# The last phase of a two-layer MetaFormer block: where its second norm and its last bias are computed

## The chip, the cores and the metric

The kernel runs on one core of a Trainium2 chip. A core has five engines with queues of their own: TensorE (PE, matmuls; PEld is its loading of weights), VectorE (DVE), ScalarE (ACT), GpSimd (POOL) and SyncE (SP, which issues the DMAs here). Each engine works through its own program in order and waits on semaphores that other engines raise. The metric is the device time of one execution in microseconds. One execution is also recorded by the hardware profiler, and all rows below are from such a record.

## The reference

Two layers on `x` of shape (8, 96, 128, 128), each a token mixer with a channel norm and a residual, then a feed-forward part with its own norm and a residual:

```python
x = x + conv(_ln_c(x))                 # layer 0 clusters, layer 1 gates with depthwise convolutions
t = _to_tokens(x)
t = t + ffn(_ln_t(t), W1, b1, W2, b2)
x = _from_tokens(t, x)

def _ln_t(v, eps=1e-5):
    m = jnp.mean(v, axis=-1, keepdims=True); s = jnp.var(v, axis=-1, keepdims=True)
    return (v - m) / jnp.sqrt(s + eps)

def _qlinear(x, W, b):                 # q_mul: round to fp8 (5 exponent, 2 mantissa bits); q_acc: to f16
    y = q_acc(jnp.einsum('bsk,nk->bsn', q_mul(x), q_mul(W)))
    return q_acc(y + q_mul(b))

def ffn(x, W1, b1, W2, b2):
    return _qlinear(jax.nn.relu(_qlinear(x, W1, b1)), W2, b2)
```

So the norm's result is rounded to fp8 before the first layer, the second layer's product is rounded to f16, and its bias is added and rounded to f16 again.

## The kernel before, in words

Three phases follow one another. Phase A is layer 0 with the norm of layer 1; phase B the depthwise convolutions of layer 1; phase C, which the change touches, finishes layer 1: the pointwise convolution, the gate, the residual, and the feed-forward part of 96 to 384 to 96 channels.

Phase C works on units. A unit is a quarter of an image, 32 rows of 128 pixels or 4096 tokens; there are 32. A unit is cut into NK = 8 groups of 512 tokens, and a group is four tiles of 128 tokens (TPC = 4). The body of every engine runs over units, and in each over nine steps s = 0 to 8. In a step two units are at work. For the unit q = i + 1, the front: `mix` (L1645, the pointwise matmul), `gate` (L1725, DVE), `turn` (L1654, transposes to tokens), `x4` (L1735, the residual), `stats` (L178, mean and variance of each token, two instructions a group). For the unit i, the back: `pe_q8` (L1476, transposes the normed fp8 tokens), `act_q8` (L296), `pe_hidden` and `act_hidden` (L348, L361, three slices of 512 columns through two PSUM buffers), `dve_hidden` (L369 three times, bias and relu; L373, the rounding to fp8), `pe_y` (L1490, three matmuls), `act_y` (L1503, out of PSUM into f16), `dve_y` (L1509, the bias), `c_turn` (L1664) and `out` (L1754, the residual sum, which goes to memory by half units).

The order on each engine is the order of the code in `body`. In a step s TensorE does q8 of group s + 1, hidden slices 0 and 1 of group s, mix of group s of the next unit, hidden slice 2, turn, c_turn and y of group s - 1. ACT does q8c of group s + 1, the three hidden copies of group s, one norm group, and y of group s - 1. DVE does relu and round of group s, gate of s, x4 of s - 1, the bias of s - 1, statistics of s - 1, out of s - 1.

The norm. For each half unit (four groups) POOL turns the variance into 1/std and -mean/std (`norm_terms`, L1794 to L1801: var, less, a power, a product). ACT applies it, four activations of 128x96 a group, with scale and bias per token (`act_norm`, L1461). The table `LN_AT` (L1430) says in which step which group is normed: groups 0 to 2 of the next unit in steps 6, 7 and 8, group 3 in step 0, groups 4 to 7 in steps 2 to 5.

Two rings of PSUM banks tie the engines. A bank of the back ring (four banks; uses in the order q8, c, y) is taken again four uses later, so y of a group waits for `out` of the group before it. A bank of the front ring (two banks; pw, turn) is taken again two uses later, so `mix` of a group waits for `gate` of the group before. The third hidden slice takes the buffer that ACT's copy of the first slice frees.

Of the kernel before, what the change touches and what calls it, by code (L numbers as in the profile page):

```python
# [5 lines left out]
F32 = mybir.dt.float32  # L6
# [175 lines left out]
def per_token(t, n):  # L182

    return t.unsqueeze(2).to_broadcast([P, n, C])


class FeedForward:
# [47 lines left out]
    def dve_y(self, dve, i, k):  # L235
        ev = self.ev

        dve.wait_ge(ev["y16"], ev.at("y16", i, k))
        y = self.y16[:, k % 2, :].rearrange("p (t c) -> p t c", c=C)
        dve.tensor_tensor(self.y16b[:, k % 2, :].rearrange("p (t c) -> p t c", c=C), y,  # L240
                          self.w["b2"][:].unsqueeze(1).to_broadcast([P, TPC, C]), ALU.add).then_inc(ev["yb"], 1)
        dve.wait_ge(ev["yb"], ev.at("yb", i, k))
        x = self.x_of(i)[:, k * CW:(k + 1) * CW]
        dve.tensor_tensor(x, x, self.y16b[:, k % 2, :], ALU.add).then_inc(ev["x2"], 1)
# [1184 lines left out]
            channels(dve, body)  # L1429


LN_AT = {6: (1, 0), 7: (1, 1), 8: (1, 2), 0: (0, 3), 2: (0, 4), 3: (0, 5), 4: (0, 6), 5: (0, 7)}
RB = H // 4


class RowFeedForward(SplitFeedForward):


    def __init__(self, nc, ctx, phase, ev, ring, xT, wts, idb):
        self.nc, self.ev, self.ring, self.xT, self.w, self.idb = nc, ev, ring, xT, wts, idb  # L1440
# [12 lines left out]
    def act_norm(self, act, i, k):
        ev = self.ev
        if k % 4 == 0:

            act.wait_ge(ev["ln2"], ev.at("ln2", i, k // 4))
            act.sem_inc(ev.passed, 1)
        x = self.x_of(i)
        for t in range(k * TPC, (k + 1) * TPC):  # L1460
# [33 lines left out]
    def act_y(self, act, i, k):  # L1494
        ev = self.ev

        act.wait_ge(ev["y_full"], ev.at("y_full", i, k))

        if k >= 2:
            act.wait_ge(ev["yb"], ev.at("yb", i, k - 2))  # L1500
        elif begun(i - 1):
            act.wait_ge(ev["yb"], ev.at("yb", i - 1, NK - 2 + k))
        act.activation(self.y16[:, k % 2, :], self.ring.bank("y", k)[0:C, 0:CH], ACT.Copy).then_inc(ev["y16"], 1)  # L1503

    def dve_y(self, dve, i, k):
        ev = self.ev

        dve.wait_ge(ev["y16"], ev.at("y16", i, k))
        dve.tensor_scalar(self.y16b[:, k % 2, :], self.y16[:, k % 2, :], self.w["b2"][:, 0:1], None,  # L1509
                          ALU.add).then_inc(ev["yb"], 1)  # L1510


def phase_c(nc, consts, pw_t, w1, b1, w2, b2, x2_dram, x3_dram, y3_dram, out_dram):
# [3 lines left out]
    with ExitStack() as ctx:  # L1517
        sb = lambda n, s, d: ctx.enter_context(nc.sbuf_tensor(n, s, d))
        sem = lambda n: ctx.enter_context(nc.semaphore(n))
        front_uses, back_uses = [], []  # L1520
        for s in range(FFN_SLOTS):
# [22 lines left out]
        less = sb("C_less", [P, NT // 2], F32)  # L1544
# [8 lines left out]
        ff = RowFeedForward(nc, ctx, "C_", ev, back, xT_flat, wts, idb)  # L1553
# [135 lines left out]
        @block.scalar  # L1689
        def _(act):  # L1690
            def body(i):
                q = i + 1
                for s in range(FFN_SLOTS):
                    if i.real and s + 1 < NK:
                        ff.act_q8(act, i, s + 1)
                    if q.real and s == NK:
                        ff.act_q8(act, q, 0)
                    if i.real and s < NK:
                        for j in range(NJ):
                            ff.act_hidden(act, i, s, j)  # L1700
                    if s in LN_AT:
                        ahead, k = LN_AT[s]
                        if (i + ahead).real:
                            ff.act_norm(act, i + ahead, k)
                    if i.real and s >= 1:
                        ff.act_y(act, i, s - 1)

            steps(act, body)

        @block.vector  # L1710
        def _(dve):
# [45 lines left out]
            def body(i):  # L1757
                q = i + 1
                for s in range(FFN_SLOTS):
                    if i.real and s < NK:  # L1760
                        ff.dve_hidden(dve, i, s)
                    if q.real and s < NK:
                        gate(q, s)
                    if q.real and s >= 1:
                        x4(q, s - 1)
                    if i.real and s >= 1:
                        ff.dve_y(dve, i, s - 1)
                    if q.real and s >= 1:
                        stats(q, s - 1)
                    if i.real and s >= 1:  # L1770
                        out(i, s - 1)

            steps(dve, body)

        @block.gpsimd
        def _(pool):
            pool.wait_ge(setup_dve, 2)

            def norm_terms(q, half):
# [4 lines left out]
                pool.sem_inc(ev.passed, 1)  # L1784
                if begun(q - 1):

                    pool.wait_ge(ev["norm2"], ev.at("norm2", q - 1, 4 * half + 3))
                    pool.sem_inc(ev.passed, 1)
# [7 lines left out]
                pool.wait_ge(ev["ln2_s"], ev.at("ln2_s", q, 3 * half + 1))
                pool.sem_inc(ev.passed, 1)
                pool.tensor_tensor(ff.rstd[:, o:o + n], var[:], expo[:, 0:n], ALU.pow).then_inc(ev["ln2_s"], 1)
                pool.wait_ge(ev["ln2_s"], ev.at("ln2_s", q, 3 * half + 2))
                pool.sem_inc(ev.passed, 1)  # L1800
# [74 lines left out]
```

## Time and profile before

| | |
|---|---|
| three runs, us | 4149.14 to 4152.14, median 4150.91 |
| the profiled execution, us | 4150.77, its span 4149.2 |
| busy, share of the span | PE 79%, DVE 73%, ACT 66%, POOL 34% |
| busy in 3300 to 3900 us of the span (inside phase C), us of 600 | PE 479.4, DVE 535.3, ACT 554.6, POOL 129.2 |
| DMA in the same stretch, share of its engines | 0.66 and 0.64 in the two halves |
| granted TensorE clock there, share of full | 0.99 in both halves |

The first three rows are of the whole program; the others show the stage that the change touches. There ACT and DVE are busy nearly all the time, and POOL about a fifth. A busy share says how much an engine does, not what it waits for; that stands in the timeline and in the waits, whose rows are below.

### The profile page before, as it was taken

How to read it: one execution, taken by the hardware profiler on the slowest of the kernel's cores; microseconds unless marked ns; L12 is line 12 of the kernel's file. 1: busy time of each engine (PE TensorE's matmuls, PEld its weight loads, DVE VectorE, ACT ScalarE, POOL GpSimd, SP SyncE). 2: the span in 40 equal slices, each digit the busy share in tenths (PEclk: the TensorE clock that was granted, in tenths of full speed). 3: DMA queues.
4: the chain of work that ended last, by engine and by line, in shares of the span. 5: the costliest groups of instructions: out<-in, count | busy, mean ns of one | idle time of the engine just before them, and what ended most of it. 6: DMA issues, size and time to landing. Idle time of an engine off the chain costs nothing. (4 is left out here: it accounts for less than half of the span.)

```text
span 4149.2 us, 80812 instructions
## 1 busy us (share of the span) xinstructions
PE 3270.8 (79%) x26660; PEld 2521.2 (61%) x26660; DVE 3025.8 (73%) x7852; ACT 2745.2 (66%) x6274; POOL 1425.2 (34%) x1892
## 2 busy tenths in 40 slices
PE   6767677776777767777659999999788778787777
PEld 5655555555555555555539999999744444444443
DVE  4888888888888888888852222222288988988987
ACT  2577777777777777777762222222189999999998
POOL 3555655556555565555420000000022222222221
PEclk8788888888888888888769999999889999999999
DMA  3133232332323323232235566566576666666662
GB/s 64 45 77 81 73 77 62 77 80 74 78 62 77 80 75 77 62 78 64 60 102 160 159 165 167 159 165 167 155 199 183 178 177 184 180 180 182 180 180 79
DMA packets 733898, 490.45 MB, mean 118 GB/s; under 512 B 420797, under 2 KB 712957, under 8 KB 721277
## 3 DMA queue, kind: packets, MB, share of 16 engines
q1 hardware_dynamic: 733564, 486.32, 44.5%
q8 instruction: 171, 2.80, 0.3%
q14 instruction: 163, 1.33, 0.1%
HBM read 284.42 MB, written 201.33 MB: 117 GB/s over the span
## 5 line engine op out<-in xcount | busy, mean ns | idle before, releaser
L1794 POOL TENSOR_SCALAR C_var<-C_st 128x16 f32<-128x16 f32 x64 | 16.3, 254 | 1697.4 <-DVE C_st L178 1697.4
L1331 PE MATMUL B_ps_row<-B_g,B_z 128*128 128x128 f32 x4608 | 555.8, 277 | 0.6 <-ACT B_g L1363 0.6
L1331 PEld LDWEIGHTS B_ps_row<-B_g,B_z 128*128 128x128 f32 x4608 | 532.1, 193 | 0.7 <-ACT B_g L1363 0.7
L361 ACT ACTIVATE A_h<-A_hid 128x512 f16<-128x512 f32 x768 | 426.5, 591 | 66.7 <-PE A_hid L348 63.1
L1424 DVE TENSOR_TENSOR B_mid<-B_ps_row,B_row_bias 128x512 f32<-128x512 f32 x192 | 132.8, 691 | 458.3 <-PE B_ps_row L1331 448.3
L166 POOL TENSOR_TENSOR A_rstd<-A_var,A_expo 128x16 f32<-128x16 f32 x128 | 454.2, 3549 | 23.7 <-POOL A_var L163 23.6
L178 DVE BATCH_NORM_STATS2 A_st<-A_xT 128x6 f32<-128x192 f32 x1536 | 443.6, 349 | 24.8 <-ACT A_xT L826 11.5
L361 ACT ACTIVATE C_h<-C_hid 128x512 f16<-128x512 f32 x768 | 426.1, 592 | 15.0 <-PE C_hid L348 7.7
L1461 ACT ACTIVATE C_q<-C_xT,C_shift,C_rstd 128x96 fp8e5<-128x96 f32 x1024 | 391.4, 456 | 40.9 <-POOL C_shift L1801 40.9
L369 DVE TENSOR_SCALAR A_hq<-A_h,A_b 128x512 f16<-128x512 f16 x768 | 250.0, 363 | 198.3 <-ACT A_h L361 193.3
L856 ACT ACTIVATE A_xc<-A_xT,A_shift,A_rstd 128x96 f32<-128x96 f32 x1024 | 379.0, 456 | 0.0
L663 PEld LDWEIGHTS A_fbank<-A_big_w,A_xq 97*128 97x128 f32 x2048 | 337.0, 236 | 63.4 <-DVE A_big_w L1098 29.5
L663 PE MATMUL A_fbank<-A_big_w,A_xq 97*128 97x112 f32 x2048 | 333.9, 318 | 23.2 <-DVE A_big_w L1098 21.7
L1375 ACT ACTIVATE B_y<-B_ps_col,B_col_bias 128x512 f32<-128x512 f32 x192 | 132.0, 687 | 318.1 <-PE B_ps_col L1342 318.1
L348 PE MATMUL A_hid<-A_q8c,A_w 96*128 96x512 bf16 x768 | 313.4, 467 | 31.6 <-ACT A_h L361 29.5
L288 PE MATMUL A_bbank<-A_w,A_hq 128*128 128x96 f16 x3072 | 218.9, 234 | 121.7 <-DVE A_hq L373 73.6
L1645 PE MATMUL C_fbank<-C_y3q,C_pw 96*96 96x512 f32 x512 | 279.5, 629 | 43.1 <-DMA C_y3q<-y_scratch 23.4
L288 PEld LDWEIGHTS A_bbank<-A_w,A_hq 128*128 128x128 f16 x3072 | 189.2, 114 | 188.4 <-DVE A_hq L373 119.3
L348 PE MATMUL C_hid<-C_q8c,C_w 96*128 96x512 bf16 x768 | 262.7, 390 | 49.9 <-ACT C_h L361 43.3
L369 DVE TENSOR_SCALAR C_hq<-C_h,C_b 128x512 f16<-128x512 f16 x768 | 243.1, 346 | 74.1 <-ACT C_h L361 67.8
L296 ACT ACTIVATE A_q8c<-A_bbank 96x512 bf16<-96x512 f32 x256 | 149.8, 586 | 192.6 <-PE A_bbank L258 191.0
L746 PE MATMUL A_fbank<-A_pabd,A_simT 128*128 128x384 f32 x512 | 234.6, 587 | 35.5 <-DVE A_xT L1050 35.5
(162 smaller groups left out, 7509.5 us busy)
## 6 DMA issues: line engine op xcount, KB each, us to landing
A_xq<-in_x SPq DMA_DIRECT2D x32, 1536.0 KB, 8.9
x_scratch<-A_xT SPq DMA_DIRECT2D x64, 768.0 KB, 3.2
x_scratch<-A_x3h SPq DMA_DIRECT2D x64, 768.0 KB, 5.4
B_z<-x_scratch SPq DMA_DIRECT2D x96, 512.0 KB, 5.0
y_scratch<-B_y SPq DMA_DIRECT2D x96, 512.0 KB, 3.7
C_x3q<-x_scratch SPq DMA_DIRECT2D x32, 1536.0 KB, 9.2
C_y3q<-y_scratch SPq DMA_DIRECT2D x32, 1536.0 KB, 15.7
C_xT<-x_scratch SPq DMA_DIRECT2D x64, 768.0 KB, 15.9
```

The costliest lines, as they stand in the source:

```text
L166: m = pool.tensor_tensor(rstd[:, o:o + n], var[:], expo[:, 0:n], ALU.pow)
L178: return dve.bn_stats(st[:, n:n + 2, :].rearrange("p t s -> p (t s)"), x[:, n * C:(n + 2) * C].rearrange("p (t c) -> p c t", t=2))
L288: m = pe.matmul(bank[:, t * C:(t + 1) * C], self.hq[:, b, s:s + P], self.w["w2"][:, j, :], start=(j == 0), stop=(j == NJ - 1))
L348: pe.matmul(self.hid2[n % 2][:], self.w["w1"][:, j * P:(j + 1) * P], self.q8c[:, k % 2, :], start=True, stop=True).then_inc(ev["hidden"], 1)
L361: act.activation(self.h16[:, k % 2, j * CH:(j + 1) * CH], self.hid2[n % 2][:], ACT.Copy).then_inc(ev["h16"], 1)
L369: r = dve.tensor_scalar(self.hq[:, b, s], self.h16[:, b, s], self.w["b1"][:, j:j + 1], 0.0, ALU.add, ALU.max)
L663: m = pe.matmul(bank[:, t * BIGN:(t + 1) * BIGN], xq[q.buf(NX)][:, n * P:(n + 1) * P], big_w[:, :], start=True, stop=True)
L746: pe.matmul(front.bank("out", k)[:, 0:CW], simT[q.buf(2)][:, k, :], pabd[:], start=True, stop=True).then_inc(ev["out_full"], 1)
L856: m = act.activation(xc3[:, k // 4, t % (NT // 2), :], xT[u.buf(NB)][:, t * C:(t + 1) * C], ACT.Identity, scale=rstd3[:, t:t + 1], bias=sh ...
L1331: m = pe.matmul(ps_row[h][:, b * P:(b + 1) * P], z[c.buf(NB)][:, h * HB + b, d:d + W], g[c.buf(2)][:, d, :], start=(d == 0), stop=(d == 2))
L1461: m = act.activation(self.q8[:, t, :], x[:, t * C:(t + 1) * C], ACT.Identity, scale=self.rstd[:, t:t + 1], bias=self.shift[:, t:t + 1], sa ...
L1645: pe.matmul(rows(front.bank("pw", k)[0:C, 0:CH]), pw[:], group(y3q[q.buf(2)], k), start=True, stop=True).then_inc(ev["pw_full"], 1)
```

## The change

In phase C the norm moves from ACT to POOL. POOL takes the mean off a group of 512 tokens (128x384, f32, into one of two buffers `xc`) and multiplies it by 1/std into the fp8 tile; two passes a group, eight a half unit, right after that half's terms. The term -mean/std is no longer computed. `LN_AT` goes. The bias of the second layer moves from DVE to ACT, right behind `act_y`. The waits follow: `act_y` no longer waits for the bias two groups back, the bias waits for ACT's own y and for `out` two groups back, and `stats` of a unit may overwrite the mean only when POOL has normed the last unit's groups of that half. The signals that POOL raised after its waits go.

```diff
-LN_AT = {6: (1, 0), 7: (1, 1), 8: (1, 2), 0: (0, 3), 2: (0, 4), 3: (0, 5), 4: (0, 6), 5: (0, 7)}
...
-        self.shift = sb("shift2", [P, NT], F32)
-    def act_norm(self, act, i, k):
...
-            m = act.activation(self.q8[:, t, :], x[:, t * C:(t + 1) * C], ACT.Identity,
-                               scale=self.rstd[:, t:t + 1], bias=self.shift[:, t:t + 1], saturate=False)
-        m.then_inc(ev["norm2"], 1)
+        self.xc = sb("xc", [P, 2, TPC, C], F32)
+    def pool_norm(self, pool, i, half):
+        ev, x = self.ev, self.x_of(i)
+        first = half * NK // 2
+        def centred(k):
+            if k >= 2:
+                pool.wait_ge(ev["norm2"], ev.at("norm2", i, k - 2))
+            elif begun(i - 1):
+                pool.wait_ge(ev["norm2"], ev.at("norm2", i - 1, NK - 2 + k))
+            t = slice(k * TPC, (k + 1) * TPC)
+            pool.tensor_tensor(self.xc[:, k % 2], x[:, k * CW:(k + 1) * CW].rearrange("p (t c) -> p t c", c=C),
+                               per_token(self.st[:, t, 1], TPC), ALU.subtract).then_inc(ev["cen2"], 1)
+        def scaled(k):
+            pool.wait_ge(ev["cen2"], ev.at("cen2", i, k))
+            if begun(i - 1):
+                pool.wait_ge(ev["q8_full"], ev.at("q8_full", i - 1, k))
+            t = slice(k * TPC, (k + 1) * TPC)
+            pool.tensor_tensor(self.q8[:, t, :], self.xc[:, k % 2], per_token(self.rstd[:, t], TPC), ALU.mult,
+                               saturate=False).then_inc(ev["norm2"], 1)
+        pool.wait_ge(ev["ln2"], ev.at("ln2", i, half))
+        centred(first)
+        for k in range(first, first + NK // 2):
+            if k + 1 < first + NK // 2:
+                centred(k + 1)
+            scaled(k)
...
         act.wait_ge(ev["y_full"], ev.at("y_full", i, k))
+        act.activation(self.y16[:, k % 2, :], self.ring.bank("y", k)[0:C, 0:CH], ACT.Copy).then_inc(ev["y16"], 1)
+    def act_y_bias(self, act, i, k):
+        ev = self.ev
+        act.wait_ge(ev["y16"], ev.at("y16", i, k))
         if k >= 2:
-            act.wait_ge(ev["yb"], ev.at("yb", i, k - 2))
+            act.wait_ge(ev["out"], ev.at("out", i, k - 2))
...
-        act.activation(self.y16[:, k % 2, :], self.ring.bank("y", k)[0:C, 0:CH], ACT.Copy).then_inc(ev["y16"], 1)
-    def dve_y(self, dve, i, k):
...
-        dve.tensor_scalar(self.y16b[:, k % 2, :], self.y16[:, k % 2, :], self.w["b2"][:, 0:1], None,
-                          ALU.add).then_inc(ev["yb"], 1)
+        act.activation(self.y16b[:, k % 2, :], self.y16[:, k % 2, :], ACT.Identity,
+                       bias=self.w["b2"][:, 0:1]).then_inc(ev["yb"], 1)
...
-                    dve.wait_ge(ev["ln2"], ev.at("ln2", q - 1, k // 4))
+                    dve.wait_ge(ev["norm2"], ev.at("norm2", q - 1, k + 3))
...
-                pool.tensor_scalar(less[:], ff.st[:, o:o + n, 1], -1.0, 0.0, ALU.mult, ALU.add).then_inc(ev["ln2_s"], 1)
...
-                pool.tensor_tensor(ff.shift[:, o:o + n], less[:], ff.rstd[:, o:o + n], ALU.mult).then_inc(ev["ln2"], 1)
...
                         norm_terms(q, half)
+                        ff.pool_norm(pool, q, half)
```

On ACT, in the middle of a unit (C_y is y out of PSUM, C_q8c the transposed tokens, C_h the hidden copies, C_q the norm's fp8 output), a step stood like this before:

```order
L1503 ACTIVATE C_y<-C_bbank 96x512
L296 ACTIVATE C_q8c<-C_bbank 96x512
L361 ACTIVATE C_h<-C_hid 128x512 x3
L1461 ACTIVATE C_q<-C_xT,C_shift,C_rstd 128x96 x4
L1503 ACTIVATE C_y<-C_bbank 96x512
```

And after, at the same place (C_y16b is y with its bias):

```order
L1516 ACTIVATE C_y<-C_bbank 96x512
L1527 ACTIVATE C_y16b<-C_y,C_b 96x512
L296 ACTIVATE C_q8c<-C_bbank 96x512
L361 ACTIVATE C_h<-C_hid 128x512 x3
L1516 ACTIVATE C_y<-C_bbank 96x512
```

The four norm activations ahead of y are gone, and one activation stands between y and the next q8c.

On POOL, one half unit of phase C before (C_var, C_rstd, C_less and C_shift are the terms of the norm):

```order
L1794 TENSOR_SCALAR C_var<-C_st 128x16
L1795 TENSOR_SCALAR C_less<-C_st 128x16
L1798 TENSOR_TENSOR C_rstd<-C_var,C_expo 128x16
L1801 TENSOR_TENSOR C_shift<-C_less,C_rstd 128x16
```

And after (C_xc is the token less its mean):

```order
L1803 TENSOR_SCALAR C_var<-C_st 128x16
L1805 TENSOR_TENSOR C_rstd<-C_var,C_expo 128x16
L1463 TENSOR_TENSOR C_xc<-C_xT,C_st 128x384 x2
L1473 TENSOR_TENSOR C_q<-C_xc,C_rstd 128x384
L1463 TENSOR_TENSOR C_xc<-C_xT,C_st 128x384
L1473 TENSOR_TENSOR C_q<-C_xc,C_rstd 128x384
L1463 TENSOR_TENSOR C_xc<-C_xT,C_st 128x384
L1473 TENSOR_TENSOR C_q<-C_xc,C_rstd 128x384 x2
```

Eight passes over 384 columns a partition follow the two small instructions that stay.

## Rows read from the trace of the kernel before

**Rows 1.** Timeline of POOL, two units: start, length, engine, line, tiles, idle before and its releaser.

```profile
3412.57 0.21 POOL L1794 TENSOR_SCALAR C_var<-C_st 128x16 f32<-128x16 f32 x1 [11.17 <-DVE C_st L178]
3412.86 0.51 POOL L1795 TENSOR_SCALAR C_less<-C_st 128x16 f32<-128x16 f32 x1
...
3416.80 0.22 POOL L1801 TENSOR_TENSOR C_shift<-C_less,C_rstd 128x16 f32<-128x16 f32 x1 [0.18 <-POOL C_rstd L1798]
...
3432.68 2.90 POOL L1798 TENSOR_TENSOR C_rstd<-C_var,C_expo 128x16 f32<-128x16 f32 x1 [0.18 <-POOL C_less L1795]
...
3447.15 0.21 POOL L1794 TENSOR_SCALAR C_var<-C_st 128x16 f32<-128x16 f32 x1 [11.17 <-DVE C_st L178]
```

**Rows 2.** Timeline of ACT: a middle step, then the end of the unit.

```profile
3432.74 1.53 ACT L1461 ACTIVATE C_q<-C_xT,C_shift,C_rstd 128x96 fp8e5<-128x96 f32 x4
3434.17 0.57 ACT L1503 ACTIVATE C_y<-C_bbank 96x512 f16<-96x512 f32 x1
3434.84 0.59 ACT L296 ACTIVATE C_q8c<-C_bbank 96x512 bf16<-96x512 f32 x1
3435.33 1.66 ACT L361 ACTIVATE C_h<-C_hid 128x512 f16<-128x512 f32 x3
...
3438.32 0.58 ACT L1503 ACTIVATE C_y<-C_bbank 96x512 f16<-96x512 f32 x1
...
3441.91 0.58 ACT L1503 ACTIVATE C_y<-C_bbank 96x512 f16<-96x512 f32 x1
...
3445.25 0.59 ACT L1503 ACTIVATE C_y<-C_bbank 96x512 f16<-96x512 f32 x1 [0.86 <-PE C_bbank L1490]
3445.75 0.58 ACT L296 ACTIVATE C_q8c<-C_bbank 96x512 bf16<-96x512 f32 x1
...
3452.18 0.59 ACT L1503 ACTIVATE C_y<-C_bbank 96x512 f16<-96x512 f32 x1 [0.82 <-PE C_bbank L1490]
```

**Rows 3.** Waits, 3020 to 4090 us: engine, line, releaser; total us, times, longest.

```profile
PE C_bbank L1476 <- ACT C_q L1461: 95.1, 122, 0.8
```

**Rows 4.** Timeline of DVE, the same middle step.

```profile
3433.26 0.56 DVE L373 TENSOR_SCALAR C_hq<-C_hq 128x1536 uint16<-128x1536 uint16 x1
3433.73 0.68 DVE L1725 TENSOR_TENSOR C_gated<-C_fbank,C_x3q 96x512 f32<-96x512 f32 x1
3434.33 0.54 DVE L1735 TENSOR_TENSOR C_xT<-C_fbank,C_xT 128x384 f32<-128x384 f32 x1
...
3435.06 0.62 DVE L178 BATCH_NORM_STATS2 C_st<-C_xT 128x6 f32<-128x192 f32 x2
3435.60 0.67 DVE L1754 TENSOR_TENSOR C_outq<-C_bbank,C_y16b 96x512 f32<-96x512 f32 x1
```

**Rows 5.** Timeline of PE, the same middle step.

```profile
3435.07 1.02 PE L1645 MATMUL C_fbank<-C_y3q,C_pw 96*96 96x512 f32 x2
3435.97 0.39 PE L348 MATMUL C_hid<-C_q8c,C_w 96*128 96x512 bf16 x1
...
3436.97 0.81 PE L1490 MATMUL C_bbank<-C_hq,C_w 128*96 128x512 f16 x3
```

**Rows 6.** Timeline: three relus beside a POOL pass (phase A), and in phase C.

```profile
757.01 1.29 DVE L369 TENSOR_SCALAR A_hq<-A_h,A_b 128x512 f16<-128x512 f16 x3
...
757.27 0.62 POOL L1164 TENSOR_TENSOR A_simr<-A_sim,A_rstd 128x256 f32<-128x256 f32 x1 [6.29 <-DVE A_sim L1014]
...
3454.71 0.86 DVE L369 TENSOR_SCALAR C_hq<-C_h,C_b 128x512 f16<-128x512 f16 x3
```

**Rows 7.** Groups of DVE, 200 to 1900 us: form, count; busy us, mean ns; idle.

```profile
L1050 DVE TENSOR_TENSOR A_xT<-A_fbank,A_xT 128x384 f32<-128x384 f32 x210 | 105.9, 546 | 0.8
...
L991 DVE TENSOR_TENSOR A_dots<-A_dots,A_rn 128x256 f32<-128x256 f32 x53 | 30.4, 574 | 1.8
...
L1014 DVE TENSOR_TENSOR A_sim<-A_sim,A_eq 128x256 f32<-128x256 f32 x52 | 22.1, 425 | 1.8
```

More of the change, by code:

```diff
@@ L1450, in __init__ @@
         self.rstd = sb("rstd2", [P, NT], F32)
-        self.shift = sb("shift2", [P, NT], F32)
-    def act_norm(self, act, i, k):
[L1454 to L1460, printed above, removed]
-            m = act.activation(self.q8[:, t, :], x[:, t * C:(t + 1) * C], ACT.Identity,
-                               scale=self.rstd[:, t:t + 1], bias=self.shift[:, t:t + 1], saturate=False)
-        m.then_inc(ev["norm2"], 1)
+        self.xc = sb("xc", [P, 2, TPC, C], F32)
[23 more added lines that the diff above has]
+            scaled(k)
     def pe_q8(self, pe, step, i, k):
@@ L1497, in act_y @@
         act.wait_ge(ev["y_full"], ev.at("y_full", i, k))
+        act.activation(self.y16[:, k % 2, :], self.ring.bank("y", k)[0:C, 0:CH], ACT.Copy).then_inc(ev["y16"], 1)
+    def act_y_bias(self, act, i, k):
+        ev = self.ev
+        act.wait_ge(ev["y16"], ev.at("y16", i, k))
         if k >= 2:
-            act.wait_ge(ev["yb"], ev.at("yb", i, k - 2))
+            act.wait_ge(ev["out"], ev.at("out", i, k - 2))
         elif begun(i - 1):
-            act.wait_ge(ev["yb"], ev.at("yb", i - 1, NK - 2 + k))
-        act.activation(self.y16[:, k % 2, :], self.ring.bank("y", k)[0:C, 0:CH], ACT.Copy).then_inc(ev["y16"], 1)
-    def dve_y(self, dve, i, k):
-        ev = self.ev
-        dve.wait_ge(ev["y16"], ev.at("y16", i, k))
-        dve.tensor_scalar(self.y16b[:, k % 2, :], self.y16[:, k % 2, :], self.w["b2"][:, 0:1], None,
-                          ALU.add).then_inc(ev["yb"], 1)
+            act.wait_ge(ev["out"], ev.at("out", i - 1, NK - 2 + k))
+        act.activation(self.y16b[:, k % 2, :], self.y16[:, k % 2, :], ACT.Identity,
+                       bias=self.w["b2"][:, 0:1]).then_inc(ev["yb"], 1)
 def phase_c(nc, consts, pw_t, w1, b1, w2, b2, x2_dram, x3_dram, y3_dram, out_dram):
@@ L1530, in phase_c @@
                 back_uses += [("c", s - 1, 0, "out", s - 1), ("y", s - 1, 0, "y16", s - 1)]
-        ev = Events(nc, ctx, "C_", dict(x1=NK, bn2=NK, ln2=2, ln2_s=6, norm2=NK, q8_full=NK, y_full=NK, c_full=NK, q8c=NK,
+        ev = Events(nc, ctx, "C_", dict(x1=NK, bn2=NK, ln2=2, ln2_s=2, cen2=NK, norm2=NK, q8_full=NK, y_full=NK, c_full=NK, q8c=NK,
                                         hidden=NJ * NK, h16=NJ * NK, relu=NK, hq=NK, y16=NK, yb=NK, out=NK, pw_full=NK,
@@ L1543, in phase_c @@
         var = sb("C_var", [P, NT // 2], F32)
-        less = sb("C_less", [P, NT // 2], F32)
         xT = [sb(f"C_xT{p}", [P, NK, CW], F32) for p in range(NB)]
@@ L1700, in body @@
                             ff.act_hidden(act, i, s, j)
[L1701 to L1704, printed above, removed]
                     if i.real and s >= 1:
                         ff.act_y(act, i, s - 1)
+                        ff.act_y_bias(act, i, s - 1)
             steps(act, body)
@@ L1765, in body @@
                         x4(q, s - 1)
-                    if i.real and s >= 1:
-                        ff.dve_y(dve, i, s - 1)
                     if q.real and s >= 1:
@@ L1783, in norm_terms @@
                 pool.wait_ge(ev["bn2"], ev.at("bn2", q, 4 * half + 3))
[L1784 to L1788, printed above, removed]
                 earlier = q if half else q - 1
@@ L1792, in norm_terms @@
                     pool.wait_ge(ev["ln2"], ev.at("ln2", earlier, 1 - half))
-                    pool.sem_inc(ev.passed, 1)
+                if begun(q - 1):
+                    pool.wait_ge(ev["norm2"], ev.at("norm2", q - 1, 4 * half + 3))
                 pool.tensor_scalar(var[:], ff.st[:, o:o + n, 2], 1.0 / C, EPS_T, ALU.mult, ALU.add).then_inc(ev["ln2_s"], 1)
-                pool.tensor_scalar(less[:], ff.st[:, o:o + n, 1], -1.0, 0.0, ALU.mult, ALU.add).then_inc(ev["ln2_s"], 1)
[L1796 to L1800, printed above, removed]
-                pool.tensor_tensor(ff.shift[:, o:o + n], less[:], ff.rstd[:, o:o + n], ALU.mult).then_inc(ev["ln2"], 1)
+                pool.wait_ge(ev["ln2_s"], ev.at("ln2_s", q, half))
+                pool.tensor_tensor(ff.rstd[:, o:o + n], var[:], expo[:, 0:n], ALU.pow).then_inc(ev["ln2"], 1)
             def body(i):
```

## The prediction

> **What bounds the kernel now.** I read the waits of the last phase first, then its timeline engine by engine. A unit (a quarter of an image, 32 of them, in nine steps s = 0..8) takes 34.58 us: the same POOL instruction recurs at 3412.57 and 3447.15 [rows 1]. In a middle step ACT never rests: four norm activations from 3432.74, the copy of y at 3434.17, the copy of q8 at 3434.84, three hidden copies from 3435.33, and after the next four norms the next y at 3438.32, 4.15 us after the last [rows 2]. The only slack in that round is that y begins at 3434.17 and q8c not until 3434.84, since TensorE had to wait for the norm: 95.1 us of such waits over 122 stops [rows 3]. So middle steps are bound by ACT, with the norm on it, and that is what the change takes away. DVE is not far behind: its step runs from the round at 3433.26 through to the end of `out` at 3436.27 in one go [rows 4].
>
> **What goes from ACT, and what is late next.** Four norm activations take 1.53 us a group and push the next instruction by 1.43 (3432.74 to 3434.17); eight groups are 11.4 us a unit. What comes back is one bias add (96x512 f16, SBUF to SBUF) behind each y. No row has it. From below, an SBUF-source activation of 96 columns pushes the next by 0.36 (1.43 over four); from above, a 512-wide copy lasts 0.59 in all, if nothing of it overlapped. I take 0.50, what one 512-wide copy pushes the next by (3445.25 to 3445.75). It waits for y16 of its own engine: between nothing and the 0.18 that POOL's waits on itself take [rows 1]; I take 0.04, near the 0.05 that a handover costs here (h begins 3435.33, lasts 0.59, TensorE goes on at 3435.97 [rows 5]).
>
> If ACT were the whole story a step would fall to about 3.2 us. It does not, because in-order TensorE and ACT form a ring that was hidden by the norm. `pe_y` (3436.97) takes 0.81; ACT's y of that step comes before q8c and the first h of the next step; TensorE's third hidden matmul waits for the buffer that this first h frees; then come turn, c_turn and the next `pe_y`. Summed [rows 2, 5]: 0.81, +0.05 handover, y 0.59, +0.04, bias 0.50, q8c to h 0.49, h 0.59, +0.05, and 1.00 from the hidden matmul through turn and c_turn to the next `pe_y` (3435.97 to 3436.97): 4.12 us. Without the bias add (y to q8c 0.50) it was 3.49 and hidden under 4.15. With the bias at 0.36 it is 3.98, with 0.59 and a wait of 0.18 it is 4.35. So the five middle steps gain 0.03 each, 0.15 a unit.
>
> At the seam of two units the norm stands alone in ACT's way: y7 at 3445.25 to the next unit's y0 at 3452.18 is 6.93 [rows 2]. There q8c, three h, a norm group, q8c and h follow one another on ACT; 1.43 goes and 0.59 + 0.04 + 0.50 - 0.50 = 0.63 comes in ahead, 0.80 less. But the first `turn` of the unit also waits for the first gate on DVE, which sits behind h and so moves 0.63 later. How much room it had I do not resolve: between 0 and 0.80 I credit half, 0.40. The step to y6 has no q8c, so its ring is 4.12 - 0.49 = 3.63; it took 3.59 (3438.32 to 3441.91). The step to y7 has neither q8c nor h ahead of it and waits for `out`, as before. I leave both at nothing. Sum without anything else: -0.55 a unit, 34.03 (with the cheapest bias add and the whole seam -1.5, with the dearest +0.75).
>
> **DVE's lost bias add.** It stood between x4 and the statistics, which wait for x4's own end. x4 to statistics was 0.73 (3434.33 to 3435.06) [rows 4]; without it the statistics start 0.54 + 0.04 after x4, so 0.15 a step is freed, less than the instruction's own length. It is off the ring, so worth nothing by itself.
>
> **What POOL takes up.** Per half unit: the third term and its wait go (one instruction of 0.51 here, one of 0.22); eight 128x384 passes come. POOL's rows give 0.22 for 16 columns [rows 1] and 0.62 for 256 undisturbed [rows 6], 1.67 ns a column, so 0.83 for 384. That the second pass writes fp8 has no POOL row; between 0.62, the 256-column pass, and twice 0.83 I take 0.83, since the width is what the rows show to count. A half is then 0.21 + 0.18 + 2.90 + 0.18 = 3.5 from var to the first pass [rows 1], and 8 x 0.83 + 2 waits of 0.18 = 7.0 us; both halves 21 of 34. The first half's burst starts in step 5 and TensorE asks for its first group in step 8; the second half's starts around the seam and is asked for in step 3. The latency is covered.
>
> **The port.** In these rows a POOL pass and certain DVE instructions exclude each other. Three relus back to back take 0.86 with POOL quiet; with a 256-column POOL pass of 0.62 beginning in their midst they take 1.29, 0.43 more [rows 6]. A DVE tensor-tensor with both inputs in SBUF has a mean of 574 against 425 for the same shape elsewhere, while one with an input in PSUM has 546 in the phase where POOL is busiest [rows 7], the 0.54 it has here [rows 4]. So gate, x4, statistics and out should not suffer; the three relus and the round should, four a step. A pass of 0.83 should cost the one it meets 0.43 + 0.21 = 0.64.
>
> The Trainium skill, "SBUF — State Buffer", section "Who interferes with whom", says that GpSimd and a VectorE instruction in a two-port mode hold the shared ports in turn, whoever starts first for the whole instruction. The trace agrees in kind (0.43 lost to a pass of 0.62); by its word a meeting costs up to the whole pass, 0.83 in place of 0.64, a full group 1.33 in place of 1.0, and the sum below would be 4220 in place of 4191.
>
> Take the start of `pe_y` as zero. The step's third h ends 0.81 + 0.05 + 0.59 + 0.04 + 0.50 + 0.49 + 1.66 = 4.14 after the last `pe_y`, so at 0.02; the last relu starts there, the round follows at 0.45 (a relu and a handover), gate is 0.92 to 1.60, x4 starts at 1.52, statistics 2.10, and out ends at 3.31 [rows 4]. The next `pe_y` needs out (3.36) and, by gate to mix to hidden (mix start to hidden 0.90 [rows 5]), 3.55. The ring needs 4.12, so DVE may be late by 0.57. The first two relus wait for the third h anyhow, so their stalls are covered; last relu and round together lose 2 x 0.64 x 0.8 (the port is held some eight tenths of a burst) = 1.0. A burst of 7.0 us spans 1.7 steps, so it meets one group of four fully (1.0) and one by half (0.5). The first half's statistics end in step 4, its burst begins some 3.8 us later (3.5, and 0.3 assumed for POOL to wake) and meets steps 6 and 7: the full group is let off only 0.08 there (3.55 + 1.0 against 3.63): +0.92, and the half group stands straight before `out` and y7: +0.50. The second half meets steps 1 and 2: 1.0 - 0.57 = +0.43, and the half group is covered. Sum +1.85 a unit. Bounds: 0 if the stalls all fall into waits, and, with four meetings of 0.64 in all four groups, 2.48 + 2.56 + 1.99 + 1.99 = +9.0.
>
> **Sum.** -0.55 + 1.85 = +1.3 us a unit, 31 full units: +40 on the profiled execution's own 4150.77 (span 4149.2, 1.6 around it; the median of the runs is 0.14 above it): 4191. Head and tail I leave at nothing: the first unit's norm waits on the same statistics, and in the last unit DVE has no gate to fall behind with.
>
> **Rivals.**
> - The port costs nothing, because DVE's stalls fall where it waited for h anyway (the ring leaves it waiting for the third h in every step). Then -0.55 x 31 = 4134, and 4104 with the cheapest bias add and the whole seam. Against it: the round follows the last relu at once and has no wait to hide in.
> - Ring, seam and port cancel: 4151. Needs a port cost of 0.3 to 0.8 a unit.
> - Every one of the four meets a pass in every group of a burst: +9.0 - 0.55 = +8.45 a unit, 4413. Speaks for it that passes follow one another closely; against it that DVE instructions issued back to back leave POOL waiting too (POOL's second small instruction lasts 0.51, its first 0.21 [rows 1]).
> - The scaled pass with its fp8 output is slow and POOL becomes the engine that sets the end. It decides from (34.6 - 2 x 4.2) / 16 = 1.64 us a pass on, 4.2 being what a half takes besides its passes; at 2.0, +5.8 a unit, 4330. Nothing in the rows speaks for a factor of two.
>
> **How the numbers follow.** Forecast (ring holds, port costs more than it gives) 0.56; free port 0.20; cancel 0.12; full collision 0.07; POOL bound 0.05. The likeliest is 4191, its own range 4160 to 4285. The range reaches down to 4120, into the free-port case, and leaves out the two heavy cases. About 0.2%, 8 us, can be told from no change: faster 0.20, same 0.12, slower 0.68.
>
> **What would show it.** Right: ACT's busy share falls by a quarter and its waits are for TensorE; `pe_y` to `pe_y` is 4.1 in steps without a burst and 4.5 or more in steps 6, 7 and 1; relu and round means rise while gate, x4 and out keep theirs; POOL passes near 0.83. Wrong: middle steps well below 4.1 (the ring is not there), relu and round at their old means (no port), or POOL waited for by TensorE.

## The result, and the profile after

| | before | after |
|---|---|---|
| median, us (runs) | 4150.89 (4149.14 to 4152.14) | 4235.02 (4233.82 to 4236.42) |
| ratio, 95% interval | | 1.0203 [1.0185, 1.0221] |
| from one y to the next, median us, y0 to y1 ... y7 to y0 | 4.09, 4.16, 4.16, 4.16, 4.16, 3.58, 3.35, 6.93 | 4.73, 4.21, 4.21, 4.21, 4.21, 4.85, 3.57, 7.28 |
| a unit, mean of 31, by `pe_y` | 34.86 | 37.50 |

The change costs 84 us, 2.64 a unit. The direction was forecast, and 4235 lies inside the range, but the forecast was +40. The steps are taken between starts of ACT's y (before) and of `pe_y` (after). After, ACT's y gives the same to 0.01; before, `pe_y` gives 3.60, 4.14, 4.16 three times, 3.58, 3.85 and 6.94, since ACT's y1 to y6 stood behind the norm, while y7 and y0 waited for `pe_y`. A unit's mean is above the sum of its medians (34.59, 37.27) because in a few units TensorE's clock falls.

Busy time of the whole program: ACT is down from 66% to 61%, POOL up from 34% to 43%, VectorE still 73%. In 3100 to 4060 us, all phase C, ACT falls from 888.6 to 688.0 us of 960, by 23%; the prediction had said a quarter.

```profile
PE 3292.5 (78%) x26660; PEld 2523.0 (60%) x26660; DVE 3106.5 (73%) x7596; ACT 2570.8 (61%) x5506; POOL 1825.2 (43%) x2276
```

ACT's timeline after, the steps to y5, y6, y7 and over the seam to the next unit's y0 (columns as in [rows 2]):

```profile
3540.00 0.59 ACT L1516 ACTIVATE C_y<-C_bbank 96x512 f16<-96x512 f32 x1 [0.82 <-PE C_bbank L1508]
3540.63 0.72 ACT L1527 ACTIVATE C_y16b<-C_y,C_b 96x512 f16<-96x512 f16 x1
3541.26 0.57 ACT L296 ACTIVATE C_q8c<-C_bbank 96x512 bf16<-96x512 f32 x1
3541.74 1.66 ACT L361 ACTIVATE C_h<-C_hid 128x512 f16<-128x512 f32 x3
3544.21 0.59 ACT L1516 ACTIVATE C_y<-C_bbank 96x512 f16<-96x512 f32 x1 [0.82 <-PE C_bbank L1508]
...
3549.07 0.59 ACT L1516 ACTIVATE C_y<-C_bbank 96x512 f16<-96x512 f32 x1 [0.82 <-PE C_bbank L1508]
...
3552.64 0.59 ACT L1516 ACTIVATE C_y<-C_bbank 96x512 f16<-96x512 f32 x1 [1.75 <-PE C_bbank L1508]
...
3559.91 0.59 ACT L1516 ACTIVATE C_y<-C_bbank 96x512 f16<-96x512 f32 x1 [1.73 <-PE C_bbank L1508]
```

Against [rows 2]: ACT now stops in every step and waits for `pe_y`, yet y to y is 4.21. The bias lasts 0.72 and q8c starts 0.63 behind it. The step from 3544.21 to 3549.07 is 4.86, the seam from 3552.64 to 3559.91 is 7.27.

DVE's timeline in the same stretch, the step that ends at y6, the undisturbed one behind it, and the seam:

```profile
3542.47 2.08 DVE L369 TENSOR_SCALAR C_hq<-C_h,C_b 128x512 f16<-128x512 f16 x3
3544.58 1.06 DVE L373 TENSOR_SCALAR C_hq<-C_hq 128x1536 uint16<-128x1536 uint16 x1
3545.57 0.68 DVE L1739 TENSOR_TENSOR C_gated<-C_fbank,C_x3q 96x512 f32<-96x512 f32 x1
...
3547.87 0.86 DVE L369 TENSOR_SCALAR C_hq<-C_h,C_b 128x512 f16<-128x512 f16 x3
3548.77 0.56 DVE L373 TENSOR_SCALAR C_hq<-C_hq 128x1536 uint16<-128x1536 uint16 x1
...
3550.43 0.63 DVE L178 BATCH_NORM_STATS2 C_st<-C_xT 128x6 f32<-128x192 f32 x2
3550.97 0.67 DVE L1768 TENSOR_TENSOR C_outq<-C_bbank,C_y16b 96x512 f32<-96x512 f32 x1
...
3556.45 1.07 DVE L373 TENSOR_SCALAR C_hq<-C_hq 128x1536 uint16<-128x1536 uint16 x1
3557.44 0.68 DVE L1739 TENSOR_TENSOR C_gated<-C_fbank,C_x3q 96x512 f32<-96x512 f32 x1
```

POOL there, the first and the last passes of one burst, then the power (the last of the norm's terms) and the first passes of the next burst:

```profile
3541.03 1.62 POOL L1463 TENSOR_TENSOR C_xc<-C_xT,C_st 128x384 f32<-128x384 f32 x2
3542.61 0.87 POOL L1473 TENSOR_TENSOR C_q<-C_xc,C_rstd 128x384 fp8e5<-128x384 f32 x1
3543.57 0.83 POOL L1463 TENSOR_TENSOR C_xc<-C_xT,C_st 128x384 f32<-128x384 f32 x1
3544.36 0.87 POOL L1473 TENSOR_TENSOR C_q<-C_xc,C_rstd 128x384 fp8e5<-128x384 f32 x1
...
3546.30 1.61 POOL L1473 TENSOR_TENSOR C_q<-C_xc,C_rstd 128x384 fp8e5<-128x384 f32 x2
...
3553.15 2.90 POOL L1805 TENSOR_TENSOR C_rstd<-C_var,C_expo 128x16 f32<-128x16 f32 x1
3556.12 2.08 POOL L1463 TENSOR_TENSOR C_xc<-C_xT,C_st 128x384 f32<-128x384 f32 x2
```

And TensorE, which stands at the mix of the burst's step, and at the first `turn` behind the seam, until DVE's gate:

```profile
3546.30 1.10 PE L1662 MATMUL C_fbank<-C_y3q,C_pw 96*96 96x512 f32 x2 [1.69 <-DVE C_gated L1739]
...
3558.26 0.52 PE L1671 MATMUL C_fbank<-C_cst,C_gated 96*128 96x96 f32 x4 [0.71 <-DVE C_gated L1739]
```

So the path is the forecast one: passes stall relus and round (2.08 + 1.06 against 0.86 + 0.56), the gate behind them is late, and TensorE in its order waits for it. Groups of the stretch 3100 to 4170 us (form, count; busy us, mean ns; idle before):

```profile
L369 DVE TENSOR_SCALAR C_hq<-C_h,C_b 128x512 f16<-128x512 f16 x684 | 285.2, 442 | 46.1 <-ACT C_h L361 36.1
...
L1473 POOL TENSOR_TENSOR C_q<-C_xc,C_rstd 128x384 fp8e5<-128x384 f32 x228 | 191.7, 850 | 0.0
...
L373 DVE TENSOR_SCALAR C_hq<-C_hq 128x1536 uint16<-128x1536 uint16 x228 | 171.3, 751 | 7.9
...
L1739 DVE TENSOR_TENSOR C_gated<-C_fbank,C_x3q 96x512 f32<-96x512 f32 x228 | 154.5, 678 | 0.0
L1768 DVE TENSOR_TENSOR C_outq<-C_bbank,C_y16b 96x512 f32<-96x512 f32 x228 | 153.2, 672 | 42.2 <-ACT C_y16b L1527 42.2
```

Before, relu had a mean of 346 and the round 560; gate and out are unchanged [rows 4]. The scaled pass with its fp8 output is no slower than the width says.

### The profile page after: what moved, and what is told of

The parts are those of the page before. It is cut to its first block and busy times, and to the rows that moved or that the text cites. A ratio compares the mean times of both kernels' runs of the same rounds, so it can differ in the third digit from the quotient of the medians.

```text
span 4232.6 us, 80166 instructions
## 1 busy us (share of the span) xinstructions
PE 3292.5 (78%) x26660; PEld 2523.0 (60%) x26660; DVE 3106.5 (73%) x7596; ACT 2570.8 (61%) x5506; POOL 1825.2 (43%) x2276
## 5 line engine op out<-in xcount | busy, mean ns | idle before, releaser
L369 DVE TENSOR_SCALAR C_hq<-C_h,C_b 128x512 f16<-128x512 f16 x768 | 321.4, 443 | 53.7 <-ACT C_h L361 42.3
L1516 ACT ACTIVATE C_y<-C_bbank 96x512 f16<-96x512 f32 x256 | 151.8, 593 | 270.5 <-PE C_bbank L1508 270.5
```

The costliest lines, as they stand in the source:

```text
L369: r = dve.tensor_scalar(self.hq[:, b, s], self.h16[:, b, s], self.w["b1"][:, j:j + 1], 0.0, ALU.add, ALU.max)
```

## The experiments

All edits are to the kernel after unless said otherwise; times are medians, each beside the kernel before on the same chip (4149.5 to 4150.4). First four kernels that take the change apart.

**Passes on 4 of 96 channels.**

```diff
+            pool.tensor_tensor(self.xc[:, k % 2, :, 0:NAR], xk[:, :, 0:NAR], ...      # NAR = 4, the scaled pass too
```

> The changed kernel, but POOL's two passes cover only 4 of the 96 channels of a token (the rest of the normed tile stays zero), so a pass is short while the order, the waits and ACT's bias add stay. Theory (port plus ring): relu and round on DVE go back to means near 345 and 560 ns, the ring of pe_y, ACT's y, bias, q8c, h and the third hidden matmul stays at 4.21 us, the first step and the step to y6 lose their excess; a unit is 34.7 to 35.1 and the time 4150 to 4168. Rival 1 (the ring alone makes the loss, port stalls are hidden): stays within 20 us of 4235. Rival 2 (TensorE is late because the norm comes late through POOL): mostly gone as well, but then TensorE must show waits for POOL in the changed kernel, which it does not.

Measured 4152.78, 1.0006 [0.9997, 1.0016]; steps 4.21 five times, 3.73, 3.47, seam 6.76. The kernel leaves out 92 of the 96 channels of the norm, but every instruction and wait is still there; only the length of the passes is gone, and with it some 81 of the 84 us. What is left of the change is worth nothing, not a gain.

**The bias back on DVE (the norm's move alone).**

```diff
-                        ff.act_y_bias(act, i, s - 1)
...
+                        ff.dve_y(dve, i, s - 1)      # between x4 and the statistics, as before
```

> Only the norm moves to POOL; the bias add goes back to DVE. Theory: the ring falls to about 3.5 and DVE sets the middle steps at 3.83; the stalls at the port stay (relu 440 to 460, round 740 ns mean, the bias add a little longer); a unit 35.2 to 36.2, time 4170 to 4205. Rival 1 (ring alone): the loss turns into a gain, 4040 to 4110. Rival 3 (port alone, the ring costs nothing): no change from 4235.

Measured 4271.56, 1.0292 [1.0275, 1.0309]: a miss, slower than the whole change. The bias add on DVE is drawn out too where it meets a pass, though not in most steps (3100 to 4060 us; shortest/median/longest ns):

```profile
L1539 DVE TENSOR_SCALAR C_y16b<-C_y,C_b x197: 335/344/756, 3101.5 to 4058.3; 96x512 f16<-96x512 f16 x197
```

The clock falls more often than after: in 23 of 31 units, which take 39.4 on average. The 8 units in which it does not fall take 37.7, against 37.27 of most units after. So of the 1.48 a unit by which this kernel is slower than after (38.98 against 37.50) about 0.5 is there without the clock, and the rest, about 1.0, is clock.

**The kernel before, with the bias on ACT (the bias's move alone).** The same lines the other way round.

> Only the bias add moves, from DVE to ACT; the norm stays on ACT. Theory: no POOL pass, so relu and round keep 346 and 560 ns; ACT is the bound and each y pushes what follows by 0.75 more (0.63 of bias, y to bias longer by 0.12), less the 0.19 a step in which ACT waited; middle steps 4.7, a unit 38.5 to 39.6, time 4275 to 4310. If ACT was not the bound before: under 4200.

Measured 4275.81, 1.0305 [1.0287, 1.0322]; middle steps 4.70, relu and round as before. ACT is the bound: busy 931.8 of 960 us (3100 to 4060). So each half alone costs about 3%, and both together 2%: the norm's move makes room on ACT for the bias, and the bias's move takes from DVE an instruction that the passes stall in some of the steps. Of the 4.12 a unit that the norm's half costs alone (38.98 against 34.86 before) some 1.0 is clock.

**c_turn ahead of the mix** (it is then out of the ring).

```diff
+                    if i.real and s >= 1:
+                        c_turn(i, s - 1)
                     if q.real and s < NK:
                         mix(i, s)
...
-                        c_turn(i, s - 1)
                         ff.pe_y(pe, i, s - 1)
```

> The changed kernel with one move on TensorE: the transposes c_turn of a group stand ahead of mix, in a place where TensorE waits for the gate, so they leave the ring and the path from gate to pe_y. Theory: 0.44 leaves both; middle steps 4.21 become 3.75 to 3.85, the first step and the step to y6 lose 0.4 each, a unit 34.5 to 35.5, time 4145 to 4180. If the middle steps are bound by something else than this ring (DVE, ACT by itself): they stay at 4.2 and the time within 20 us of 4235.

Measured 4245.25, 1.0224 [1.0206, 1.0241]. The ring is confirmed (middle steps 3.78 to 3.97 in place of 4.21), the time is a miss: the steps with a burst are 5.17 and 5.44, the seam 7.53. TensorE, done sooner, waits the longer for the gate (up to 2.3 us), and its granted clock falls: 38 stretches at the lower level (1.2 GHz), 147 us in all, 7 in the kernel after.

**The same, with c_turn repeated in those waits** (4, 6 and 4 times in steps 2, 7 and 8; the result is the same bank written again).

```diff
-                        c_turn(i, s - 1)
+                        c_turn(i, s - 1, {2: 4, 7: 6, 8: 4}.get(s, 1))
```

> As e4_cturn, but in steps 2, 7 and 8 the four transposes of c_turn are done 4, 6 and 4 times over with the same result, so that TensorE works where it waited for DVE's gate. Theory (the shorter ring of e4_cturn was paid back by TensorE's clock, which fell to half in 39 stretches of 155 us together, 17 in the step to y6 and 16 at the seam): the stretches at half clock fall below a third, a unit from 38.2 to 35.5 to 37, time 4150 to 4215. Rival (the pay-back is DVE being late, the clock is a symptom): the clock stays up and the time stays within 15 us of 4245.

Measured 4207.61, 1.0136 [1.0119, 1.0152]: more work, 38 us less. The stretch 3100 to 4060 us with c_turn first, then filled (its length; busy us of PE, PEld, DVE, ACT, POOL; granted clock, share of full; DMA share, GB/s):

```profile
3100.00:4060.00 960.00, 775.00 (x4024) 420.93 (x4023) 862.85 (x1808) 676.57 (x1209) 508.37 (x504) 0.94 0.60 166
```

```profile
3100.00:4060.00 960.00, 870.72 (x5315) 535.12 (x5313) 882.35 (x1875) 700.10 (x1251) 525.83 (x522) 1.00 0.62 172
```

One stretch at the lower level is left, the seam is 6.84, and 5.13 and 5.44 remain: those are the port.

Then kernels that keep the whole passes and place them. Every group's two passes wait for DVE's round of one step, so that they lie beside gate, x4, statistics and out.

```diff
-        pool.wait_ge(ev["ln2"], ev.at("ln2", i, half))
...
+        ahead, after = {0: (1, 6), 1: (1, 7), 2: (1, 7), 3: (0, 0), 4: (0, 1), ...}[k]
...
+        pool.wait_ge(ev["hq"], ev.at("hq", i - ahead, after))
+        centred(k)
+        scaled(k)
```

The terms of the second half now come behind group 3.

**Placed, nothing else.**

> The changed kernel, with POOL's passes spread out: each group's two passes wait for DVE's round of a step (groups 0 to 2 in steps 6, 7, 8, group 3 in step 0, groups 4 to 7 in steps 1 to 4), so that they lie beside gate, x4, statistics and out, which do not use the shared port. Nothing is computed differently. Theory (port): relu and round return to means near 350 and 560 ns, the ring stays 4.21, a unit 34.9 to 35.3, time 4148 to 4170. Rival (what costs is POOL's work as such, or its late norm): stays near 4235, and TensorE waits for the norm.

Measured 4174.68, 1.0052 [1.0035, 1.0069], slightly above what was expected: the step y1 to y2 is 4.80, all others are those of the narrow passes. Group 3 follows the round of step 0, where DVE has nothing but the gate before the next relus, and the terms of the second half come late.

**Placed, and the bias later on ACT**, behind the first hidden copy of the next step, out of the ring.

```diff
                         for j in range(NJ):
                             ff.act_hidden(act, i, s, j)
+                            if j == 0 and s >= 2:
+                                ff.act_y_bias(act, i, s - 2)
...
```

> As e5_paced, and ACT's bias add of a group moves behind the first hidden copy of the next step, so that it no longer stands in the ring (y, q8c, h, third hidden matmul, turn, c_turn, y). Theory (ring): the ring falls by 0.65 to about 3.55, out on DVE then waits some 0.4 for the bias and sets the middle steps at 3.75 to 3.95; a unit 32.4 to 34, time 4065 to 4120. If the clock of TensorE falls in the longer pauses, part is given back. If the ring were not the bound: 4150 to 4170 as e5_paced.

Measured 4175.75, 1.0057 [1.004, 1.0074]: a miss. Middle steps fall to 3.96, but y1 to y2 is 5.07, and in 14 units the clock falls there.

**The same, with c_turn ahead of the mix.**

> As e6_paced_late, and c_turn stands ahead of mix on TensorE. Theory: the ring is no longer the bound in e6_paced_late (DVE is), so little changes: within 20 us of it, unless TensorE's clock falls more often as it waits longer in one piece, as in e4_cturn.

Measured 4156.1, 1.0014 [1.0004, 1.0023]: 20 us less than without it, just within what was expected, but still no gain over before. DVE's and POOL's timelines behind the seam show why:

```profile
3520.60 1.86 DVE L369 TENSOR_SCALAR C_hq<-C_h,C_b 128x512 f16<-128x512 f16 x3
...
3525.34 2.12 DVE L369 TENSOR_SCALAR C_hq<-C_h,C_b 128x512 f16<-128x512 f16 x3
```

```profile
3520.16 0.98 POOL L1462 TENSOR_TENSOR C_xc<-C_xT,C_st 128x384 f32<-128x384 f32 x1 [4.42 <-DVE C_hq L373]
...
3525.32 0.83 POOL L1462 TENSOR_TENSOR C_xc<-C_xT,C_st 128x384 f32<-128x384 f32 x1
```

Group 3's passes (from 3520.16) meet the relus of step 1; the power behind them ends late, and group 4's (from 3525.32) begin together with the relus of step 2. In step 8, where DVE has no relu and waits, there was room. So the groups were placed anew: group 0 behind the round of step 6, 1 to 3 behind that of step 7 and on through step 8, then the second half's terms, and 4 to 7 behind the rounds of steps 1 to 4 of their own unit (the expectation of the kernel with c_turn ahead of the mix, below, counts the first two steps one too high).

```diff
+        ahead, after = {0: (1, 6), 4: (0, 1), 5: (0, 2), 6: (0, 3), 7: (0, 4)}.get(k, (1, 7))
```

**New placing alone.**

> After with the new placing of POOL's groups alone; nothing else of the change is touched. Theory (the whole loss of 84 us is passes that meet relus and roundings): as the kernel whose passes were narrowed to 4 channels: relu .35, round .56, middle steps 4.21, unit 34.9 to 35.1, time 4148 to 4160, no difference from before. Rival (a full pass costs VectorE something in gate, x4 or statistics too, or late groups make TensorE wait): 4165 or more.

Measured 4153.51, 1.0007 [0.9998, 1.0016]; steps 4.21 five times, 3.73, 3.47, 6.76, to the hundredth those of the narrow passes. Relu and round in 3100 to 4060 us, of the kernel after and of this one (count: shortest/median/longest ns):

```profile
L369 DVE TENSOR_SCALAR C_hq<-C_h,C_b x614: 332/353/990, 3105.3 to 4059.8; 128x512 f16<-128x512 f16 x154
L373 DVE TENSOR_SCALAR C_hq<-C_hq x204: 559/561/1070, 3106.8 to 4056.6; 128x1536 uint16<-128x1536 uint16 x102
```

```profile
L369 DVE TENSOR_SCALAR C_hq<-C_h,C_b x659: 333/353/355, 3099.7 to 4057.9; 128x512 f16<-128x512 f16 x165
L373 DVE TENSOR_SCALAR C_hq<-C_hq x220: 559/560/561, 3100.5 to 4058.3; 128x1536 uint16<-128x1536 uint16 x110
```

With 43% of POOL's time still busy, no relu and no round is stalled. The 81 us were neither POOL's work nor the waits for it, but where its passes fell.

**New placing and the late bias.**

> The new placing with the ACT bias one step later, c_turn in its old place. Theory (ring shortened by the bias and its push, about .6 a step, until VectorE or the other ring bounds): middle steps 3.95 as in the paced kernel with the late bias, y1 to y2 without the stalled 5.07, unit 33.4 to 34.3, time 4090 to 4130. Rival (what the middle steps give, the seam takes back, since the unit is bound by VectorE's 3.35-us steps and ScalarE's sum): unit 34.7 to 35.0, time 4140 to 4155.

Measured 4123.27, 0.9933 [0.9919, 0.9946]: faster than the kernel before by 27 us. ACT's middle step, with the bias behind the first hidden copy:

```profile
3512.15 0.59 ACT L1516 ACTIVATE C_y<-C_bbank 96x512 f16<-96x512 f32 x1 [0.86 <-PE C_bbank L1508]
3512.64 0.58 ACT L296 ACTIVATE C_q8c<-C_bbank 96x512 bf16<-96x512 f32 x1
3513.12 0.59 ACT L361 ACTIVATE C_h<-C_hid 128x512 f16<-128x512 f32 x1
3513.59 0.72 ACT L1527 ACTIVATE C_y16b<-C_y,C_b 96x512 f16<-96x512 f16 x1
3514.20 1.08 ACT L361 ACTIVATE C_h<-C_hid 128x512 f16<-128x512 f32 x2
3516.11 0.59 ACT L1516 ACTIVATE C_y<-C_bbank 96x512 f16<-96x512 f32 x1 [0.83 <-PE C_bbank L1508]
```

y to q8c is 0.49 again, the step 3.96. The unit is 33.96. DVE and TensorE in the same step show what holds it there:

```profile
3514.42 0.69 DVE L1773 TENSOR_TENSOR C_outq<-C_bbank,C_y16b 96x512 f32<-96x512 f32 x1 [0.17 <-ACT C_y16b L1527]
...
3515.25 0.82 PE L1508 MATMUL C_bbank<-C_hq,C_w 128*96 128x512 f16 x3
```

The bias has left one ring and stands in another: y, q8c, h, the bias (ends 3514.31), `out` right behind it, `pe_y` behind `out`, and the next y at 3516.11.

**And c_turn ahead of the mix.**

> After, with POOL's groups placed anew: groups 0 and 1 follow VectorE's rounding of steps 7 and 8 of the unit before (there is no rounding in step 8 for the next step to meet), 2 and 3 are done in the same idle step, 4 to 7 follow the rounding of steps 1 to 4 of their own unit; and with both cures of the ring (the ACT bias one step later, behind the first hidden copy; c_turn ahead of the mix). Theory (what was left of the loss in the paced kernels, 24 us, is one group's passes that still met the relus of step 1, and the terms of the second half run in the middle of step 2): no step is longer than 4.0, mean relu .35, round .56, unit 33.4 to 34.0 against 34.87 of before, time 4095 to 4130: the first kernel of this study that is faster than before. Rival A (the norm waits on VectorE, so groups become late for TensorE): a wait of TensorE for the norm in most units, 4150 to 4180. Rival B (the clock falls in the longer pauses at the seam as in the kernel with c_turn first): 20 or more low-clock stretches of 3.4 us, unit 34.6 to 35.2, time 4140 to 4165.

Measured 4124.88, 0.9938 [0.9925, 0.9952], within the forecast, but no better than without: the seam is 6.97 in place of 6.73, and the clock falls there in nearly every unit (27 of 29 stretches in the last two steps). Three units in which it does not fall take 33.53, against 33.96 with c_turn in its old place, and those in which it falls 34.2: the clock takes back what the place gives.

**New placing, the bias on DVE**, the fourth corner.

> The new placing of POOL's groups with the second layer's bias back on VectorE (where it was before): the norm's move alone, as in the kernel that put the bias back, but with passes that meet neither relus nor roundings. It is the fourth corner beside after, the bias put back, and the placing alone. Theory (the earlier loss of the norm's move by itself, 4272, was passes that met relus and rounding and the clock that fell in the pauses; ScalarE's .50 to .63 of norm or bias is then out of the ring y, q8c, h, third hidden, c_turn, pe_y): relu .35, round .56, middle steps 3.6 to 3.9 where VectorE with .34 more a step is the bound, seam 6.0 to 6.9, unit 33.0 to 34.3, time 4092 to 4133, so that the norm's move is worth 20 to 60 us by itself and the bias's move costs what the placing alone (4153.5) lies above this. Rival A (VectorE, 73 % busy, is the bound with the bias on it, and passes now are late for TensorE): unit 34.8 or more, 4148 or more. Rival B (clock): 15 or more low-clock stretches, 4130 to 4165.

Measured 4173.2, 1.0055 [1.0041, 1.0069]: a miss, slower than with the bias on ACT by 20. Relu and round are clean; the bias is not (same columns):

```profile
L1539 DVE TENSOR_SCALAR C_y16b<-C_y,C_b x214: 337/981/986, 3105.1 to 4058.0; 96x512 f16<-96x512 f16 x107
...
  PE C_bbank L1508: 80.9, 107
```

In most steps the add, f16 from SBUF to SBUF, starts with a pass and takes 0.98 in place of 0.34, `out` behind it is late, and TensorE waits for `out` (the second row: total us, times). The two steps from y2 to y4 are 4.47 in place of 4.21. One meeting costs 0.64, which is what the prediction had put on it. The stall is not the whole of the 20 us: units come in turn with 35.00 and 36.67 (35.81 on average, 34.98 with the bias on ACT), and in the longer ones the clock falls behind y7, where the seam is 7.38 in place of 6.21 (16 stretches in phase C, one with the bias on ACT). So the clock, a rival in the expectation, is in it too; no run parts the two.

## Why the prediction was right or wrong

The narrow passes give the change without its port, and the kernel after less that one the port alone:

| us a unit | forecast | measured |
|---|---|---|
| y0 to y5, ring | -0.15 | +0.32 |
| steps to y6 and y7 | 0 | +0.27 |
| seam | -0.40 | -0.17 |
| port: first step, to y6, to y7, seam | +0.43, +0.92, +0.50, 0 | +0.52, +1.12, +0.10, +0.52 |
| clock | not counted | -0.04 |
| sum | +1.3 | +2.6 |

(Measured: sums of the step medians; clock: what is left to the means, 37.50 less 34.86. Before, and after, TensorE's clock falls in 7 stretches of these 31 units, so this nearly cancels.)

- The mechanism held. Middle steps are bound by the ring, 4.21 for 4.12. Relu and round are stalled, gate, x4, statistics and `out` are not; POOL's passes last 0.83 undisturbed; TensorE never waits for POOL. That DVE's freed add is worth nothing by itself no run tests alone.
- **The step that failed is the first sum, -0.55.** It measured +0.42, and makes 0.97 of the 1.3 a unit that are missing, 30 us; the sum of the port makes the other 0.41, 13 us. Its term "0.50, what one 512-wide copy pushes the next by" for the bias is too small, and so is the upper bound of 0.59: it lasts 0.72 and pushes by 0.63 (3540.63 to 3541.26). That alone turns the ring from 4.12 to 4.25, over the 4.16 that the norm had set. The step to y6 was "left at nothing", though its ring was given as 3.63 against 3.59; with 0.13 more it is 3.76, and 3.73 came. The step to y7 is 0.12 longer counted from ACT's y, but from `pe_y` to `pe_y` it falls from 3.85 to 3.47: y6 no longer stands behind a norm, so the step counted from it begins sooner. `out` in that step follows the statistics (3550.43, 3550.97) and waits for no bias. (The sum's cheapest case leaves out the ring's own 0.15: it is -1.65, which gives 4100 and not 4104.)
- The seam's credit of 0.40 for "between 0 and 0.80" was 0.17 without the port. With it, it is a loss of 0.35: the forecast let the second burst begin clear of the seam, but the variance starts as soon as the last statistics are done, the passes at 3556.12, and the unit's first round (1.07) stands in their way. The gate behind it is late, and `turn` waits 0.71.
- **The port** came to 2.26 for 1.85. "1.0" for a full group, counted as the forecast counts it, from the end of the third h to the gate, is 1.27: 2.17 after (3543.40 to 3545.57) against 0.90 with the narrow passes (3541.44 to 3542.34, below). The passes leave hardly a gap, and three of the four instructions meet one (2.08 + 1.06 less 1.42 is 1.7 in all; what falls before the end of the third h is covered, as forecast). So the two meetings count nearly whole, and the "0.8" of them was too small. "Let off only 0.08" came near: 0.15, which makes +1.12 for +0.92. The half group's +0.50 was +0.10: the burst ends at 3547.91 as the next relus begin, and they and their round are undisturbed. The seam's +0.52 was not forecast. The price of a meeting was right (0.64 for the bias above; 1.22 for the two in 2.08). The Trainium skill, "SBUF — State Buffer", section "Who interferes with whom", would have up to the whole pass, 0.83; here the median bias, which starts with the pass, loses 0.64. Which instructions a burst meets, and that one meets the seam, follows from no price, only from the times at which each burst begins.

```profile
3539.78 1.66 ACT L361 ACTIVATE C_h<-C_hid 128x512 f16<-128x512 f32 x3
...
3542.34 0.68 DVE L1743 TENSOR_TENSOR C_gated<-C_fbank,C_x3q 96x512 f32<-96x512 f32 x1
```

- Of the rivals, the free port is what the new placing shows, and it ends at no change (4153.5), not at 4134, for the reason in the second point.

What is not settled: how much of the 0.5 a unit that the kernel with the bias back on DVE and unplaced passes (4271.56) loses to after without the clock is the drawn-out bias, and what the stall and the clock each take of the 20 us in the fourth corner. No run parts these.

## What to carry to other kernels

Work moved to POOL is not free because POOL is idle: look at which of VectorE's instructions run on 16-bit data from SBUF to SBUF, and put the passes beside the others; here that placing was worth 81 us and the move itself nothing. When the longest engine in a step is relieved, sum the ring of handovers that it hid before crediting anything, and put what is added outside that ring (27 us faster than before, with the same instructions). Time saved on TensorE can come back as a lower clock, so look at the granted clock of each step and compare the units with and without a fall, not only the means.

## What the runs showed of the hardware that was not expected

- An activation from SBUF with a bias, 96x512 f16 to f16, lasts 0.72 and pushes the next by 0.63, where the same width from PSUM lasts 0.59 and pushes by 0.49.
- A 96x512 f16 add on VectorE that starts with a POOL pass takes 0.98 in place of 0.34, a 128x512 relu 0.99 in place of 0.35, the round of 128x1536 1.07 in place of 0.56; instructions with f32 or PSUM operands beside the same passes keep their length.
- With c_turn ahead of the mix TensorE's granted clock falls to the lower of its levels in 38 stretches, though its longest wait there (3100 to 4060 us) is 2.3 us; filling the waits with repeated transposes left one stretch and took 38 us off the whole kernel.
